# Attention over a node graph: GpSimd clamps a whole key tile in one instruction instead of two half tiles

## What is computed

```
h = jnp.maximum(_layernorm(x, axis=-1), 0.0)
q = (embeds[rows] @ qW).reshape(e, HEADS, dh)
k = (embeds[cols] @ kW).reshape(e, HEADS, dh)
v = (embeds[cols] @ vW).reshape(e, HEADS, dh)
scores = jnp.clip(jnp.einsum('ehd,ehd->eh', q, k), -10.0, 10.0)
exp_s = jnp.exp(scores)
norms = jax.ops.segment_sum(exp_s, rows, num_segments=nvar)[rows]
w = exp_s / (norms + 1e-08)
res = jax.ops.segment_sum(w[:, :, None] * v, rows, num_segments=nvar).reshape(nvar, d)
```

## Time and profile before

| | us |
|---|---|
| median of 3 runs | 1166.79 |
| the profiled execution: span from first to last instruction | 1161.5 |
| what lies around the span | 5.3 |
| attention, first score to the write of the last block | 412.7 to 789.4 |
| before it: edge counts, scans, degrees and projections | 0 to 412 |
| behind it: graph propagation and the last layer | 791 to 1161.5 |

### The profile page before, as it was taken

How to read it: one execution, slowest core, us unless ns; L and a number is a source line. 1 busy time by engine, 2 the same in 40 slices (tenths; PEclk the granted TensorE clock), 3 DMA queues, 4 the chain that set the end, 5 groups by cost and what they waited for, 6 DMA issues and landing times.

```text
span 1161.5 us, 23065 instructions
## 1 busy us (share of the span) xinstructions
PE 1003.2 (86%) x8302; PEld 612.5 (53%) x8302; DVE 876.5 (75%) x1318; ACT 608.1 (52%) x824; POOL 492.1 (42%) x522
## 2 busy tenths in 40 slices
PE   3887777777778779999999999996999699999995
PEld 2554455554544423223223333333669599999984
DVE  8668888888765569999999999997846654543366
ACT  7455556565563579898989898881100000001132
POOL 8434443343310069999999999980000000000000
PEclk9788999896897979999999999997999799999997
DMA  0010000000001631222222223221001100010111
GB/s 9 25 44 8 10 6 5 6 5 8 17 1 50 202 82 44 62 50 63 48 59 51 64 58 72 51 65 48 1 1 42 42 25 24 2 35 11 57 45 42
DMA packets 98715, 44.63 MB, mean 38 GB/s; under 512 B 85006, under 2 KB 96526, under 8 KB 98482
## 3 DMA queue, kind: packets, MB, share of 16 engines
q1 hardware_dynamic: 96914, 41.43, 13.4%
q0 software_dynamic: 1696, 1.74, 0.6%
HBM read 30.58 MB, written 12.56 MB: 37 GB/s over the span
## 4 chain that ended last, share of the span: by engine, by line
PE 77%; issue 9%; DVE 7%; ACT 3%; DMA 1%; POOL 1%; SPq 1%; DVEq 0%; ACTq 0%; POOLq 0%
PE PS L1298 18%; PE PS L1062 12%; PE PS L551 11%; PE PS L1072 11%; PE PS L555 8%; PE PS L1306 3%; PE PS L1773 3%; PE PS L1051 3%; ACT Eb L1114 2%; PE PS L1289 1%; POOL Eb L975 1%; DVE Eb L1134 1%; PE PS L875 1%; DMA kd<-QH 1%; PE PS L1759 1%
## 5 line engine op out<-in xcount | busy, mean ns | idle before, releaser
L1114 ACT ACTIVATE Eb<-PS,small 128x1024 f32<-128x1024 f32 (+4 forms) x350 | 333.3, 1003 | 45.0 <-PE PS L1062 40.3
L1134 DVE TENSOR_TENSOR Eb<-Eb,PS 128x2048 f32<-128x2048 f32 (+4 forms) x175 | 341.8, 2011 | 18.8 <-POOL Eb L975 10.1
L975 POOL TENSOR_SCALAR Eb<-Eb 128x1024 f32<-128x1024 f32 (+4 forms) x350 | 318.9, 935 | 76.7 <-ACT Eb L1114 73.2
L589 ACT ACTIVATE CT<-PS 128x500 f32 x313 | 183.7, 587 | 142.5 <-PE PS L555 134.3
L551 PE MATMUL PS<-mov,oneS 128*128 128x100 f16 x1565 | 183.3, 228 | 78.8 <-issue 74.7
L551 PEld LDWEIGHTS PS<-mov,oneS 128*128 128x128 f16 x1565 | 145.4, 105 | 158.4 <-issue 112.6
L1298 PE MATMUL PS<-hs,CT 128*128 128x192 f16 (+1 forms) x2500 | 213.3, 247 | 3.6 <-DVE SG L1539 1.6
L1298 PEld LDWEIGHTS PS<-hs,CT 128*128 128x128 f16 (+1 forms) x2500 | 207.9, 99 | 7.3 <-DVE SG L1539 2.3
L1062 PE MATMUL PS<-Qb,Kb 96*128 96x512 f16 (+3 forms) x700 | 180.4, 362 | 13.7 <-DMA Kb<-kd 10.8
L435 DVE TENSOR_TENSOR oneS<-iotaX,KL 128x2560 f16<-128x2560 int16 x80 | 120.4, 1505 | 70.3 <-PE PS L555 67.8
L1072 PE MATMUL PS<-Eb,V 128*25 128x512 f32 (+3 forms) x1400 | 166.7, 548 | 0.8 <-DVE Eb L1134 0.8
(11 more groups left out here) (281 smaller groups left out, 905.9 us busy)
## 6 DMA issues: line engine op xcount, KB each, us to landing
Kb<-kd SPq DMA_DIRECT2D x168, 96.0 KB, 2.3
qd<-QH SPq DMA_DIRECT2D x12, 192.0 KB, 2.7
kd<-QH SPq DMA_DIRECT2D x12, 192.0 KB, 3.1
hs<-t_d SPq DMA_DIRECT2D x12, 192.0 KB, 2.5
Qb<-qd SPq DMA_DIRECT2D x4, 384.0 KB, 3.8
CT<-x_d SPq DMA_DIRECT2D x1, 1200.0 KB, 7.1
x_d<-B SPq DMA_DIRECT2D x6, 192.0 KB, 1.9
t_d<-A SPq DMA_DIRECT2D x6, 192.0 KB, 1.8
```

The costliest lines, as they stand in the source:

```text
L589: a.activation(K.CT[:, :, bass.ds(words[g % 4][0], GI * W)], K.bank(g % 4)[:, 0:25 * GI * W].rearrange("p (a c) -> p a c", a=25), ACT.Copy ...
L975: g.tensor_scalar(e, e, EHI, ELO, ALU.min, ALU.max).then_inc(S("clamped"), 1)
L1114: a.activation(e, ps, ACT.Exp, scale=K.unsc[0:r, :]).then_inc(S("score_exp"), 1)
L1134: v.tensor_tensor(e, e, cn, ALU.mult).then_inc(S("weighed"), 1)
```

## The change

The two clamps of an iteration become one instruction over all four heads. It waits for the second exponential (`score_exp` at 2 it + 2) and signals once, so the weighing waits for it + 1 signals in place of 2 it + 2. Nothing else differs.

```
-        for k in range(2):
-            e = K.Eb[0:r, it % NE_, 2 * k:2 * k + 2, 0:wb]
-            g.wait_ge(S("score_exp"), 2 * it + k + 1)
-            g.tensor_scalar(e, e, EHI, ELO, ALU.min, ALU.max).then_inc(S("clamped"), 1)
+        e = K.Eb[0:r, it % NE_, :, 0:wb]
+        g.wait_ge(S("score_exp"), 2 * it + 2)
+        g.tensor_scalar(e, e, EHI, ELO, ALU.min, ALU.max).then_inc(S("clamped"), 1)
         if it % FETCH == FETCH - 1 and it // FETCH < NT:
             gamma(g, K, it // FETCH)
-    g.wait_ge(S("clamped"), 2 * len(ITS))
+    g.wait_ge(S("clamped"), len(ITS))
...
         e = K.Eb[0:r, it % NE_, :, 0:wb]
-        v.wait_ge(S("clamped"), 2 * it + 2)
+        v.wait_ge(S("clamped"), it + 1)
         v.tensor_tensor(e, e, cn, ALU.mult).then_inc(S("weighed"), 1)
```

## The result

The changed kernel takes 1178.14 us (median of 4 runs, 1174.67 to 1179.63) against 1166.84 (4 runs, 1166.59 to 1169.49): slower by 0.93%, ratio 1.0093, 95% interval 1.0076 to 1.0109. The profiled execution has a span of 1175.3 us in place of 1161.5, 13.8 more. The spans differ by more than the medians because the profiled execution of before was a quick one: the changed kernel's took 1177.36 us, 2.1 more than its span, and in every run of the experiments the time is 1.7 to 2.1 above the span. So the 5.3 us in the table of the time before are not what lies around the span; some 2 of them are (an estimate by these runs), and the other 3 are the distance of that execution from the median.

What follows compares the result with a forecast made beforehand. TensorE and ScalarE were taken to pace each other at 2.285 us an iteration; gathers 0.3, first four boundaries 4.6, last two 1.0 and the end 0.5 sum to 6.4 us, giving 1173.2 us, range 1168.8 to 1179.5.

Steps and rivals of the forecast that it cites:

- the dearer clamp: Rival, 20%: GpSimd's whole clamp costs more than its sizes' line says, or gathers hold GpSimd longer; 1175.5 to 1181 us.
- late clamp: On GpSimd the whole clamp, 1.90 us, starts only behind the second exponential; behind a gather the weighing starts 0.72 us later.
- spent cushion: The 0.69 us between weighing's end and TensorE's waiting count is used up; VectorE's lateness then costs 0.6 us per wide-block boundary.
- blocked addition: At a block's boundary VectorE's two-SBUF-input addition (L1157) waits for the running GpSimd clamp: 1.2 us for 0.66, 0.55 more.
- the 5.3 us around the span: Time outside the profiled span, added unchanged to the forecast span of 1167.9 us to give 1173.2 us.
- best lag: Shortest time from an iteration's second exponential's end to its weighing's start: 1.23 us before the change, 2.09 after.
- Behind a gather: In wide blocks the weighing's 0.72 us delay is hidden but for 0 to 0.03 per gather; 0.3 us for all 25.
- signs that I had named: Among others: VectorE waits for GpSimd in most iterations; GpSimd's idle time for ScalarE is many times what it was.
- The boundaries: Between attention blocks: 1.15 us at each of the first four, 4.6 in all; fifth 0.6, sixth 0.4.
- The end: Behind the last iteration nothing hides the later clamp; weighing, value, sums and HBM write move by 0.54, taken as 0.5 us.
- the boundaries cost less: Rival, 20%: the addition meets gaps between clamps, or slack takes more of the delay; 1.0 to 4 us remain, 1167.8 to 1171.
- GpSimd as the pacer: Rival, 5%: GpSimd paces the attention stage; VectorE's 10.1 us of waits for it could be won, reaching 1156.7 us.

Runs made afterwards that it cites:

- Experiment 7: The kernel before without its 25 gathers, what they bring being set to 1: 1166.90 us, ratio 1.0004 to before.
- experiment 2: The changed kernel with the boundary's product written back into PSUM, so the addition has only one SBUF input: 1167.94 us, ratio 1.0017 to before.
- experiment 3: The kernel before with the boundary's product written back into PSUM, so the addition reads it there: 1163.55 us, ratio 0.9976 to before.
- experiment 1: The changed kernel timed again without any edit: 1177.68 us, ratio 1.0099 to before.
- experiment 4: The kernel before with both half clamps waiting for the second exponential, not merged: 1174.55 us, ratio 1.0071 to before.
- experiment 6: The changed kernel without its 25 gathers, what they bring being set to 1: 1173.97 us, ratio 1.0068 to before.
- experiment 8: The kernel before with two VectorE copies of 512 elements from PSUM added behind each boundary's addition: 1183.41 us, ratio 1.0135 to before.

## Why the prediction was right, point by point

The forecast was 1173.2 with a range of 1168.8 to 1179.5; measured were 1178.14, slower as forecast, in the range and 4.9 above the point. The time lies in the band that I had given to the dearer clamp (1175.5 to 1181), and the clamp was not dearer; so that it fell inside the range is in part luck. The mechanism (late clamp, spent cushion, blocked addition) was right, and a price was missing.

The forecast's sum carries the 5.3 us around the span, which are 3 us too many; as the 1161.5 was too low against the median by the same 3 us, the 1173.2 does not change.

**The clamp and the lag.** Forecast 1.90, 1.47 and 1.25 us and a best lag of 2.09; measured 1897, 1473 and 1255 ns and 2.08 (without gathers the kernel before reaches 1.22, for 1.23). The dearer clamp, my first rival, is out.

**Behind a gather** no more than 0.03 us were to be lost, with the count 0.06 behind the weighing's end. It starts 0.06 behind; in the earlier trace rows it stood 0.75 behind. The loss is small and still larger than forecast: 0.23 us for the three gathers ahead of iteration 22 (50.95 against 50.72). Experiment 7 shows that the same gathers are hidden in full before. Two of the signs that I had named did not come: VectorE waits for GpSimd 33 times and not in most iterations, and GpSimd's waits for ScalarE are 111.5 us against 73.2, not many times as much (50 against 18 if only the stretch from 430 to 780 us is taken).

**The boundaries.** Forecast 1.15 for each of the first four. The blocks grew by 1.17, 2.69, 2.48 and 1.64 us; less 1.6 for each of the two falls they are 1.17, 1.1, 0.9 and 1.6, 4.8 in sum against 4.6. At the first, 0.35 of it lies at the copy of bank 4, 0.70 at the addition, and 0.1 behind two gathers. The longer wait of the addition was put at 0.55 and is 0.53 at the first (1.61 against 1.08), then 0.44, 0.55 and 0.65; experiment 2 takes it out and most of the loss with it. The fifth boundary cost 0.67 against 0.6. The sixth cost 1.6 against 0.4: before, L1157 met the end of a clamp there and took 0.52 us, after it took 1.53.

**The end.** 0.5 forecast; from the first score of iteration 172 to the last value the stage grows by 0.53.

**The mis-sized term** is the boundary's. I sized it by VectorE's lateness and the addition's wait, and put the granted clock at nothing without a word. The runs showed in its place the same two and, behind stops of TensorE of 1.8 us, two falls of the granted clock; the iterations behind them take 1.63 and 1.58 us more than those behind the first boundary, 3.2 us in all. The sixth boundary costs 1.2 more than forecast. With these the sum is 6.4 + 3.2 + 1.2 = 10.8 us against 11.0 measured in the stage. By the experiments the 10.3 us of the six blocks are some 3.2 of clock, 3.8 of lateness (experiments 2 and 3) and the rest, 3.3, of the addition's wait, whose six lengthenings add up to 3.5.

**The other rivals.** That the boundaries cost less is out by the same rows. GpSimd as the pacer is out by experiment 7: without gathers VectorE's waits for GpSimd fall from 10.1 to 4.7 us and the time is the same; and with 29.5 us less work on GpSimd the kernel is slower.

## What to carry to other kernels

Merging two instructions saves an engine's time, but it lengthens the way from producer to consumer by the part that ran beside the producer, here 0.85 us. Before merging, find the cushion of whoever waits last in the chain, at the places where it is already spent (block boundaries), rather than the busy share of the engine. Where work comes in lumps on an engine that has nearly no slack, spread the lumps over the iterations: here that was worth 5.6 us with half clamps and some 12 with whole ones.

## What the hardware showed that I had not expected

**Stops and the granted clock.** TensorE's stops at boundaries, with what follows, in eight profiled kernels: of the stops of 0.7 to 1.09 us (before, after, experiments 1, 2, 4, 6 and 7) none was followed by a fall; nor were those of 1.32 and 1.42 us in the narrow blocks; of nine stops of 1.79 or 1.80 us (after, experiments 1 and 6) seven were followed at once by 3.4 us at 0.50; of five of 2.2 to 2.6 us (experiment 8) four were, two of them with 6.8 us (there the fall starts 0.3 us before the stop ends: at 674.10, with the count at 674.38). One stop of 1.33 us in experiment 8 was followed by a fall too, so the length of the stop alone does not decide it. Ahead of the stop of 1.80 us that ended at 553.67 in the changed kernel, TensorE had been busy for 37.9 of the 38 us from 496 to 534, at a granted clock of 1.00. Why the first boundary of the changed kernel, with the same stop of 1.79, had no fall in two profiles and had one in experiment 6 stays open, and so does what decides it.

**An addition with two SBUF inputs and a clamp on GpSimd hold each other up.** In the kernels before and after, the addition of 384 columns ended 0.41 us behind the running clamp, whether that was a half of 0.83 or 1.04 us or a whole one of 1.47 or 1.90 (0.31 for 288 columns), and the half clamp that started next took 1.32 us in place of 1.04. The other way round, in experiment 4 two additions that started 0.08 us before a clamp's end took 0.56 us, and the clamp behind them 1.41 and 1.42. At the fifth boundary of before, the addition met the last 0.02 us of one half clamp and ended 0.30 behind the next one. The weighings, with one input in PSUM, ran beside clamps at 2.27 to 2.29 us throughout, and so did the addition at 0.55 once it read PSUM. The Trainium skill says in "SBUF — State Buffer", section "Who interferes with whom", that a VectorE instruction with two SBUF inputs contends with a GpSimd instruction that reads SBUF, and one with at most one SBUF input, outside the two-port modes, does not; the trace agrees. What this case adds is the price: the longer the clamp, the longer the addition beside it (0.52 to 1.11 us in the kernel before, 1.41 to 1.61 in the kernel after).
